# A fused convolution and mixture-of-experts block on one core: a 3x3 convolution in plain fp32 on four 64x64 tiles, and new orders of the work around it

## What is computed

```python
x = x + conv0(ln_c(x))         # 1x1 to 32 channels, norm, pair products, 1x1 to 64
t = tokens(x)                  # one row of 64 channels per pixel
t = t + ffn0(ln_t(t))          # 2 of 8 experts per image, 64 -> 128 -> 64, layer norm
x = image(t)
x = x + conv3x3(ln_c(x), w)/9  # 64 to 64 channels, zero padding 1
t = tokens(x); z = ln_t(t)
logits = z @ Wg + bg           # per pixel
w = softmax of the 2 best of 8 logits, 0 elsewhere
for e in range(8):             # dense over the experts
    t = t + w[:, e] * (gelu(z @ W1[e] + b1[e]) @ W2[e] + b2[e])
```

## Time and profile before

| | us |
|---|---|
| median of three runs | 315.68 (315.27 to 315.76) |
| profiled execution, its own time | 312.68 |
| its span, first to last instruction | 310.9 |
| PE busy | 286.3 (92%) |
| DVE busy | 173.1 (56%) |
| ACT busy | 169.7 (55%) |
| granted PE clock, mean | 0.997 |

### The profile page before, as it was taken

One profiled execution on the slowest core, in us unless ns is written; L12 is line 12 of the kernel. 1 busy time (PEld: TensorE's weight loads), 2 busy tenths in 40 slices (PEclk: granted clock), 3 DMA queues, 4 the chain that ended last, 5 costly groups with the idle time before them and its releaser, 6 DMA issues.

```text
span 310.9 us, 6417 instructions
## 1 busy us (share of the span) xinstructions
PE 286.3 (92%) x2368; PEld 147.5 (47%) x2368; DVE 173.1 (56%) x404; ACT 169.7 (55%) x328; POOL 35.6 (11%) x74
## 2 busy tenths in 40 slices
PE   6999999998888986988999999999999999999993
PEld 4465353366653543975867334533333333333441
DVE  3576967885522469778983365853333344433533
ACT  3632236225367555334434665566677777777772
POOL 8125546100153000000000000000000000000000
PEclk9999999999999999999999999999999999999998
DMA  7636868620000000000003994000079910700100
GB/s 206 232 82 185 223 191 237 205 112 2 0 0 3 0 0 3 0 2 0 3 0 57 212 207 77 2 0 2 11 155 225 200 34 1 171 0 2 26 13 17
DMA packets 11566, 24.09 MB, mean 77 GB/s; under 512 B 2192, under 2 KB 4400, under 8 KB 11408
## 3 DMA queue, kind: packets, MB, share of 16 engines
q1 hardware_dynamic: 9808, 19.19, 25.1%
q0 software_dynamic: 1328, 3.84, 4.9%
q10 hardware_dynamic: 400, 0.66, 0.8%
HBM read 14.73 MB, written 1.33 MB: 52 GB/s over the span
## 4 chain that ended last, share of the span: by engine, by line
PE 71%; DVE 13%; ACT 8%; issue 5%; DMA 1%; DVEq 1%; ACTq 0%; POOLq 0%
PE PS L785 20%; PE PS L763 18%; PE PS L717 6%; PE PS L592 5%; PE PS L497 4%; PE PS L527 2%; PE PS L671 2%; PE PS L609 2%; PE PS L544 2%; PE PS L581 2%; DVE D L1286 2%; PE PS L557 2%; ACT amp L934 1%; PE PS L689 1%; PE PS L616 1%
## 5 line engine op out<-in xcount | busy, mean ns | idle before, releaser
L763 PE MATMUL PS<-N,late 64*64 64x512 f32 (+1 forms) x640 | 77.7, 549 | 0.0
L934 ACT ACTIVATE amp<-PS,late 128x512 f32<-128x512 f32 (+1 forms) x80 | 47.2, 640 | 22.4 <-PE PS L763 22.0
L934 ACT ACTIVATE h<-PS,late 128x512 f32<-128x512 f32 (+1 forms) x80 | 47.2, 641 | 18.0 <-PE PS L763 17.5
L763 PEld LDWEIGHTS PS<-N,late 64*64 64x64 f32 x640 | 26.5, 133 | 33.7 <-issue 32.0
L785 PE MATMUL PS<-h,late 64*64 64x512 f32 (+1 forms) x320 | 39.5, 556 | 1.5 <-DVE D L1286 0.9
L785 PE MATMUL PS<-amp,late 64*64 64x512 f32 (+1 forms) x320 | 39.2, 552 | 0.7 <-ACT amp L934 0.3
L1286 DVE SCALAR_TENSOR_TENSOR D<-PS,late,moved 128x512 f32<-128x512 f32 (+1 forms) x24 | 14.8, 658 | 33.6 <-PE PS L785 31.5
L1286 DVE SCALAR_TENSOR_TENSOR D<-PS,late,img 128x512 f32<-128x512 f32 x16 | 11.3, 746 | 34.9 <-PE PS L785 34.9
L1292 DVE TENSOR_TENSOR X<-D,X 128x512 f32<-128x512 f32 (+1 forms) x40 | 25.4, 634 | 2.1
L497 PE MATMUL PS<-X,early 128*128 128x384 f32 x48 | 20.5, 543 | 2.8 <-DMA X<-x_in 1.5
L395 POOL DMA_DIRECT2D moved<-amp x40 | 19.7, 497 | 27.6 <-DMA moved<-amp 12.9
(11 more groups left out here) (153 smaller groups left out, 327.2 us busy)
## 6 DMA issues: line engine op xcount, KB each, us to landing
img<-gates_hbm SPq DMA_DIRECT2D x4, 1024.0 KB, 13.8
moved<-amp SPq DMA_DIRECT2D x40, 96.0 KB, 3.3
moved<-amp POOLq DMA_DIRECT2D x35, 96.0 KB, 2.9
moved<-gates_hbm SPq DMA_DIRECT2D x4, 512.0 KB, 7.6
moved<-gates_hbm SPq DMA_DIRECT2D x2, 1024.0 KB, 9.6
late<-late_in SPq DMA_DIRECT2D x1, 1852.0 KB, 7.6
moved<-gates_hbm SPq DMA_DIRECT2D x4, 256.0 KB, 5.6
mix<-mix_in SPq DMA_DIRECT2D x1, 897.0 KB, 9.1
```

Source lines behind the costliest of these rows:

```text
L763: mm = pe.matmul(PS[64 * r:64 * r + 64, 2 * (n % RING) + half, 0:w], L("w1")[rows, u:u + 64], N[rows, a:a + w], start=True, stop=True, ski ...
L934: act.activation(hid(n, half)[:, 0:w], PS[:, 2 * (n % RING) + half, 0:w], ACT.Gelu, bias=L("b1")[:, BLOCKS * g + b:BLOCKS * g + b + 1]).th ...
```

## The change

- The convolution is computed in plain fp32. LN3's vector step writes straight into `img`, which now holds the two images of a pair on the two halves of the partitions. There are four steps, one per pair, each nine taps of four 64x64 matmuls with 288 columns, one on each quarter of the array. DVE adds the result to X in three operations. The split of weights and image, ACT's part and the separate addition are gone.
- The second gate buffer no longer shares memory with `img`, and SP's wait for the convolution ahead of the second span's loads is gone.
- `logits` has three steps for each half. The first half's gates are turned in one step into another bank (`turn_all`).
- In the second mixture hidden and down steps come two and two, and ACT's gelu takes both banks in one instruction. PE's semaphore is raised once per step.
- The three lists have new orders: LN4's first half and the first mixture steps come ahead of LN3's second half and of the last two convolution steps.

```diff
-CONV_PAIR = [1, 2, 1, 2, 3, 3, 3, 3]
+CONV_PAIR = [1, 2, 3, 3]
...
-TURN_BANK = [[4, 5, 4], [7, 6, 7]]
+TURN_BANK = [7, 6, 7]
...
 def second_mixture():
...
-    out = [(n / 2, ("hidden", *at[n])) for n in range(STEPS)] + [(n / 2 + 0.74, ("down", *at[n])) for n in range(STEPS)]
-    return sorted(out, key=lambda o: o[0])
+    out = [("hidden", *at[n]) for n in range(2)]
+    for n in range(0, STEPS, 2):
+        out += [("hidden", *at[k]) for k in range(n + 2, min(n + 4, STEPS))] + [("down", *at[k]) for k in (n, n + 1)]
+    return out
...
     "PE": """
...
-        center 2 3, down0 3 1, spread 3 0, spread 3 1, spread 3 2, center 2 4, center 2 5, root 2 1, conv 0, conv 1, spread 2 3, conv 2, conv 3, center 4 0,
-        spread 2 4, spread 2 5, center 4 1, center 4 2, center 3 3, root 4 0, center 3 4, center 3 5, root 3 1, spread 4 0, unread 7, spread 4 1, unread 2,
-        spread 3 3, unread 2, spread 4 2, spread 3 4, spread 3 5, unread 5, logits 0, unread 1, conv 4, mix 2, conv 5, turn 0 0, turn 0 1, turn 0 2, conv 6,
-        mix 2, conv 7, mix 3, center 4 3, center 4 4, mix 2, center 4 5, mix 2, root 4 1, mix 7, spread 4 3, mix 4, spread 4 4, spread 4 5, mix 4, logits 1,
-        mix 7, turn 1 0, mix 8, turn 1 1, mix 8, turn 1 2, mix 111,
+        center 2 3, down0 3 1, spread 3 0, spread 3 1, spread 3 2, center 2 4, center 2 5, conv 0, root 2 1, conv 1,
+        center 4 0, spread 2 3, spread 2 4, center 4 1, center 4 2, spread 2 5, center 3 3, root 4 0, center 3 4, center 3 5, unread 2, root 3 1, unread 3,
+        spread 4 0, spread 4 1, logits 0 0, spread 4 2, logits 0 1, logits 0 2, mix 7, turn_all, mix 5, spread 3 3, spread 3 4, spread 3 5, conv 2,
+        conv 3, mix 2, center 4 3, center 4 4, mix 2, center 4 5, mix 4, root 4 1, mix 6, spread 4 3, mix 2, spread 4 4, spread 4 5, mix 4,
+        logits 1 0, logits 1 1, logits 1 2, mix 8, turn 1 0, mix 8, turn 1 1, mix 8, turn 1 2, mix 104,
...
     "ACT": """
...
+        moments 4 0, moments 4 1, moments 4 2, moments 3 3, moments 3 4, moments 3 5, mix 2, gate 0 2, mix 6,
+        moments 4 3, moments 4 4, mix 1, moments 4 5, mix 9, gate 1 2, mix 62,
...
     "DVE": """
...
+        spread 3 0, spread 3 1, spread 3 2, conv 0, root 2 1, conv 1, spread 2 3, spread 2 4,
+        spread 2 5, root 4 0, spread 4 0, spread 4 1, spread 4 2, gate 0 0, gate 0 1, gate 0 2, gate 0 3, turn_all, root 3 1, spread 3 3, spread 3 4, spread 3 5,
+        conv 2, conv 3, mix 1, root 4 1, mix 1, spread 4 3, spread 4 4,
         spread 4 5, mix 1, gate 1 0, gate 1 1, gate 1 2, gate 1 3, mix 2, turn 1 0, mix 1, turn 1 1, turn 1 2, mix 14,
...
+        img = sb("img", [128, PAIRS, PADN])
+        gB_odd = sb("gB_odd", [128, EXP * 512])
...
             gates_over_channels(0)
-            sp.wait_ge(conv_mm, 2 * PAIRS)
             gates_over_channels(1)
...
+            def conv(p):
...
+                elif p == 2:
                     pe.wait_ge(LN[3]["normed"], NCH)
                 else:
+                    pe.wait_ge(x3_done, p)
+                w = L("conv").rearrange("p (t o) -> p t o", t=TAPS)
+                iv = img[:, p, :].rearrange("p (y z) -> p y z", z=PADW)
+                for tap in range(TAPS):
+                    dy, dx = tap // 3, tap % 3
+                    for half in range(2):
+                        q = slice(64 * half, 64 * half + 64)
+                        for j in range(2):
+                            o = 64 * (half ^ j)
+                            mm = pe.matmul(PS[o:o + 64, 2 * CONV_PAIR[p] + j, 0:HALFPIX], w[q, tap, :],
+                                           iv[q, j * ROWS + dy:j * ROWS + dy + ROWS, dx:dx + WD],
+                                           start=tap == 0, stop=tap == TAPS - 1, skip_group_check=True)
                 mm.then_inc(conv_mm, 1)
...
+            def turn_all():
+
+                pe.wait_ge(gt, GT_ALL)
+                pe.wait_ge(LN[3]["copied"], NCH)
+                for t in range(GTILES):
+                    mm = pe.matmul(PS[32 * (t % 3):32 * (t % 3) + 32, GROUP_BANK[1], t // 3 * TILE:(t // 3 + 1) * TILE],
+                                   gw_flat[:, 2 * EXP * t:2 * EXP * (t + 2)], E("ident"), start=True, stop=True, skip_group_check=True)
+                mm.then_inc(gT_mm, 3)
...
+                act.wait_ge(f1_mm, n + 1)
+                act.activation(h2[n // 2 % 2][:, 2 * (n % 2):2 * (n % 2) + 2, 0:w], pair(n % RING, w), ACT.Gelu,
+                               bias=L("b1")[:, BLOCKS * g + b:BLOCKS * g + b + 1]).then_inc(f1_act, 1)
...
+                elif i == 3:
+
+                    ve.wait_ge(img0, 1)
+                    for p, y0, ny in pieces(c):
+                        a, n = p * PIX + y0 * WD, ny * WD
+                        iv = img[:, p, :].rearrange("p (y z) -> p y z", z=PADW)
+                        last = ve.tensor_tensor(iv[:, 1 + y0:1 + y0 + ny, 1:1 + WD],
+                                                PS[:, ln_bank(3, c), a - c * BANK:a - c * BANK + n].rearrange("p (y z) -> p y z", z=WD),
+                                                D[:, a:a + n].rearrange("p (y z) -> p y z", z=WD), ALU.mult)
+                    last.then_inc(LN[3]["normed"], 1)
...
+            def conv(p):
+
+                ve.wait_ge(conv_mm, p + 1)
+                for j in range(2):
+                    a = p * PIX + j * HALFPIX
+                    for lo, hi in ([(0, 128)], [(0, 64), (64, 128)])[j]:
+                        o = 64 * j - lo if j else 0
+                        last = ve.scalar_tensor_tensor(out=X[lo:hi, a:a + HALFPIX], in0=PS[o:o + hi - lo, 2 * CONV_PAIR[p] + j, 0:HALFPIX],
+                                                       scalar=1.0 / TAPS, in1=X[lo:hi, a:a + HALFPIX], op0=ALU.mult, op1=ALU.add)
+                last.then_inc(x3_done, 1)
```

More of the change, by code:

```diff
@@ L214, in order @@
 def order(engine):
-    mix = iter([step for _, step in second_mixture()
+    mix = iter([step for step in second_mixture()
                 if engine == "PE" or (engine == "ACT" and step[0] == "hidden")
@@ L342, in build @@
         LN = [{k: sem(f"ln{i}_{k}") for k in
[L343 removed]
+               ("centered", "squared", "copied", "summed", "rooted", "inverted", "spread", "normed")}
               for i in range(5)]
@@ L720, in conv, with logits @@
                 mm.then_inc(conv_mm, 1)
-                if 2 * k == 4:
-                    spare.append((4, conv_a, n + 1))
-            def logits(g):
+                if CONV_PAIR[p] == 2:
+                    spare.append((4, x3_done, p + 1))
+            def logits(g, k):
                 pe.wait_ge(late_ld, 16)
-                pe.wait_ge(conv_a, 4 * (g + 1))
-                pe.wait_ge(LN[4]["normed"], GCH * (g + 1))
-                for t in range(GTILES * g, GTILES * (g + 1)):
+                pe.wait_ge(x3_done, PAIRS // GROUPS * (g + 1))
+                pe.wait_ge(LN[4]["normed"], GCH * (g + 1) if g else k + 1)
+                for t in tiles(GCH * g + k):
@@ L791, in _ @@
                     "route_picks": route_picks, "weights": weights, "bias": bias, "unread": unread, "warm": warm, "hidden0": hidden0,
-                    "down0": down0, "conv": conv, "logits": logits, "turn": turn, "hidden": hidden,
+                    "down0": down0, "conv": conv, "logits": logits, "turn": turn, "turn_all": turn_all, "hidden": hidden,
                     "down": down}
@@ L831, in root_ @@
                         load_table(ACT.Exp)
-            def parts(i, c):
-                if i != 3:
-                    return
-                act.wait_ge(LN[i]["normed"], c + 1)
-                act.wait_ge(img0, 1)
-                for p, y0, ny in pieces(c):
-                    a = p * PIX + y0 * WD
-                    for half in range(2):
-                        q = slice(64 * half, 64 * half + 64)
-                        iv = img[q, PAIRS * half + p, :].rearrange("p (y z) -> p y z", z=PADW)
-                        last = act.activation(iv[:, 1 + y0:1 + y0 + ny, 1:1 + WD],
-                                              N[q, a:a + ny * WD].rearrange("p (y z) -> p y z", z=WD), ACT.Copy)
-                last.then_inc(LN[i]["high"], 1)
             def amplify(c):
@@ L909, in hidden0 @@
                                bias=w2b1sel[:, 2 * (2 * p + half) + k, CH:CH + 1]).then_inc(f0_act, 1)
-            def conv(n):
-                p, half = n // 2, n % 2
-                act.wait_ge(conv_mm, n + 1)
-                act.activation(icols(clow, p, 64 * half, 64 * half + 64),
-                               pair(CONV_PAIR[n], HALFPIX, 64 - 64 * half, 128 - 64 * half), ACT.Copy,
-                               scale=1.0 / TAPS).then_inc(conv_low, 1)
             def gate(g, k):
@@ L931, in hidden @@
                     act.wait_ge(f1_out, n - HELD + 1)
[L932 to L939 removed]
+                act.wait_ge(f1_mm, n + 1)
+                act.activation(h2[n // 2 % 2][:, 2 * (n % 2):2 * (n % 2) + 2, 0:w], pair(n % RING, w), ACT.Gelu,
```

(9 more changed lines are left out.)

111 lines of the change are left out of this document (26 added, 85 removed).

## The result

The changed kernel takes 321.66 us, median of 4 runs, against 315.48 for the kernel before: a ratio of 1.0213, 95% interval 1.0139 to 1.0287. The forecast was 319.8, range 315.2 to 324.0, slower with 0.74. The profiled execution took 320.2 (span 318.4); before's took 312.68, so the traces are 7.5 us apart.

The account below looks back on a forecast made before the run. PE was taken to bound the kernel. Work -6.6 and waits +7.4 gave +0.7 us, two clock falls +3.4, together +4.1 on the profiled 312.68: 316.8, plus 3.0 to the median, 319.8 (range 315.2 to 324.0).

Parts of the forecast that it names:

- The waits: PE idle at conv 3 and four mixture down steps until DVE frees banks: 1.8, 3.2, 5.1, 2.35 and 4.1 us.
- The walk: Count through the PE, ACT and DVE queues, old and new: waits +7.4, work -6.6, together +0.7 us, ending at 307.6.
- the rival that rested on it (315.1): Changes of tile form cause the 1.3 us shortfall and the new convolution removes it: 315.1, not slower, chance 0.16.
- The convolution: On PE, 0.483 us a group, 4.35 per image pair, 17.4 in all: 3.9 us less than the old one.
- Both rivals on it: Strided image slows tiles, 0.59 a group, 323.6 with falls, chance 0.08; row tiles in one bank alternate, 0.97, 337, 0.04.
- The turns: In the mixture, old waits of 2.8 us at team changes and 3.5 in the last span go.
- The clock: Falls from 2.4 to 1.2 GHz behind two long PE waits, 1.7 us each: +3.4; bounds nothing and four at 2.9.
- D8: Mixture down step 8 on PE, behind root 4 1: waits 5.1 us for DVE's team 1 products, clock fall expected.
- D16: Mixture down step 16 on PE: waits 4.1 us while DVE does second gates before team 3's products, clock fall expected.
- 1.93 and the clock held: Old profile: longest wait among the steps that change, 1.93 us at PE's root 2 1, brought no clock fall.
- the clock holds: Rival: 5 us waits with full work on both sides might not lower the clock; 316.4, give or take 1, chance 0.18.
- before's 3.0: Old kernel's median taken as 3.0 us above its profiled execution and added to 316.8, giving 319.8.

Follow-up runs that it names:

- the flat read: Changed kernel, each convolution matmul reading 288 adjacent columns of the padded image instead of 12 rows of 24: 322.39 us in one run.
- team 0's products first: Changed kernel with the first four mixture steps' products ahead of conv 2 on DVE, PE's and ACT's lists adjusted: 317.37 us, ratio 1.0115.

## Why the prediction was right, point by point

- **The number** came closer than its terms, and that is luck. The profiled execution took 320.2 and not the 316.8 forecast, 3.4 more; the median lies 1.5 above it and not 3.0, which takes 1.5 back, so the median is 1.9 off. As a change it is +6.2 between the medians and +7.5 between the traces, for +4.1. The mechanism was right: the waits eat what PE's work gives, and falls of the clock make the loss.
- **The waits** were right in place, releaser and size: forecast 1.8, 3.2, 5.1, 2.35 and 4.1 (with hand-overs), measured as idle time 1.59, 3.04, 4.97, 2.19 and 3.75. Moving the products on DVE's list, with PE's steps to match, took each away.
- **The walk** gave +0.7. Its shortfall against the trace was 1.3 in the old order. After: the last addition ends at 314.79 + 0.94 = 315.73, the walk said 307.6, 8.1 less. Of that 0.65 came before the point where it starts (center 2 3 at 117.47, 116.82 before; the kernel before, run again, is 0.6 late there too), 0.5 is the convolution, 5.3 the clock: 1.7 left. So the shortfall did not go away, and the rival that rested on it (315.1) falls.
- **The convolution** was mis-sized a little, 0.5 us in all. Its groups take 0.488 for 0.483; conv 0 and conv 1 take 4.53 a pair (0.503 a group) for 4.35, most of it with the change to the next step's form, which the walk leaves out in both orders. conv 2 and conv 3, with DVE's wait behind them, came nearly as walked: 6.19 and 7.63 to the next start for 6.15 and 7.55. Both rivals on it fall: the flat read is no faster, and 0.97 for two row tiles in one bank is far off. The Trainium skill, TensorEngine Tiling (Gotcha 1: PSUM Pressure), says that different row tiles cannot access one bank at the same time; here two do, each in its half of the partitions, at 0.488 to 0.503, so the measurement decides against reading it as a turn-taking.
- **The turns** gave what was forecast in the new order: the window from 222 to 292 has no idle time at team changes, one gelu alone takes 1.11 us, as forecast, and the last span's steps of two groups take 0.86 to 0.92. On the old order alone they gave 3 to 4.5 for 5.7.
- **The clock** is the term that was too small: 3.4 for two falls. The two places were right, and not by luck: in every trace that keeps D8's wait (five) or D16's (five) a fall follows. Too small were the size of D16's fall and the term of nothing for the first hidden steps. In the profiled execution D8 lost 1.7 (1.55 + 0.16 on the next two groups), D16 2.8 (1.72 + 1.06: the fall lasted up to the turn at 222.49), and the unforecast one 0.8 (5.19 - 4.39): 5.3. The sum for the traces is then 0.65, the walk's 0.7, 0.5 and 5.3, together 7.2 of the 7.5 measured; the walk's larger shortfall is the rest.
- **The step "1.93 and the clock held"** was too firm: in another execution it fell behind the same wait. Behind waits of this size, and behind D4's and D12's, a fall comes in some executions and not in others, which one trace can't show.
- **The rival "the clock holds"** falls, since falls show in the windows behind both long waits; of the shorter ones it was right in part.
- **Carrying over before's 3.0** between profile and median was not sound: before's profiled execution had escaped a fall that other runs of it have. Before moved to 315.48 and then to 313.6 to 315.0 in the later comparisons, and the changed kernel's median is 1.5 above its profiled execution. The same spread makes the 0.2% that a measurement was said to tell from no change too small: the interval of the result is 0.7% to either side.
- **The early gates** came later than walked (turned at 153.59, on DVE until 155.1) and landed in time all the same: DVE did not wait for them, and with team 0's products first it had them at 162.88.

## What to carry to other kernels

When an engine's list is shortened or reordered, walk the other engines' lists against it: here each wait could be read beforehand from the place of one DVE step, and putting four steps of products earlier (with two groups shifted at each of two places on PE) turned a loss of 2% into a gain of 4.2 to 4.8%. Price a clock fall as a range over several executions and not as one number from one trace. In these runs fillers paid inside waits (1.9 us less) and outside them cost what they saved; removing the waits gave far more.

## What the runs showed of the hardware

- Over all traces of this case, a fall of the granted clock follows some waits of PE every time and others now and then (by the starts of the steps behind the wait, as above):

| place | PE's wait ahead, us | traces with it | with a fall |
|---|---|---|---|
| D8 | 4.96 to 4.97 | 5 | 5 |
| D16 | 3.75 to 3.76 | 5 | 5 |
| D4 | 3.04 | 6 | 3 |
| D12 | 2.18 to 2.19 | 7 | 1 |
| root 2 1 and the first convolution, old order | 1.93 to 1.94 | 3 | 1 |
| conv 3 | 1.59 to 1.60 | 6 | 0 |
| conv 2 | 0.74 | 9 | 2 |
| first hidden steps, behind the narrow logits | under 0.45 | 10 | 8 |

- So the same step behind the same wait falls in one execution and holds in another. The Trainium skill, TensorE: Matmul & The Clock Gate (Part 1), says that what it watches is not aligned with the program, so that the count of slowed matmuls differs between runs of one kernel; the traces are of that kind, 1.00 and 0.74 between 147 and 153 us with the same lists up to there.
- A fall cost 0.8 to 3.1 us in these traces, 1.3 to 2.0 in most. In the changed kernel's four runs the mean granted clock was 0.967 to 0.977, and the two at 0.967 are the slowest (322.56 and 323.14).
